# One PixArt-style chain on one core: normalisation, key/value and maxima steps moved in two hand-written turn tables

## The chip, the core and the metric

The kernel runs on one core of a Trainium2 chip. The metric is the device time of the whole program in microseconds; three runs of the kernel before took 2682.87, 2684.73 and 2690.53 us, the median is 2684.73. TensorE (PE) multiplies into PSUM, VectorE (DVE), ScalarE (ACT) and GpSimd (POOL) work beside it, and SyncE (SP) issues the DMAs. Each engine runs its own instructions in order and waits on semaphores for the others.

## The reference

The input x is (16, 256, 256): 16 samples of 256 tokens with 256 features, with a context of 120 tokens per sample and a condition vector. Four layers follow one another. Layers 0, 2 and 3 are full transformer blocks; layer 1 is a cross-attention alone. All is fp32, with 16 heads of 16 features:

```
full layer:                                       layer 1:
  shift, scale, gate = silu(cond) @ W_mod + b       q = (ada_ln(x) @ Wq + bq)
  x += gate * proj(self_attention(mod(ln(x))))      k, v = ada_ln(ctx) @ Wkv + bkv
  x += cproj(cross_attention(ln(x), ctx))           x += softmax(q k^T / 4) v @ Wp + bp
  x += gate * fc2(gelu(fc1(mod(ln(x)))))
```

In layers 1 and 3 the context is normalised before its keys and values are made; in 0 and 2 it is not. Layer 2 has a gain and a bias in the norm ahead of its cross-attention.

## The kernel before, in words

The weights of a layer and all of x stay in SBUF. The work is cut by layer and sample and laid out as a pipeline of jobs. The parts of a job are:

- **P**: normalise x (N, A), transpose it (LN), make q, k and v for self-attention (Q, K, V). RES adds a bias to x on GpSimd.
- **F**: self-attention. S0 to S3 compute scores, and VectorE takes each row's maximum from them (`row_max_F`, line 858). X splits the maxima in two parts, M transposes them on TensorE and ScalarE copies them out (`max_t_F`, line 983). T0 to T3 compute the scores again the other way round with the maxima subtracted, and ScalarE exponentiates (`probs`, line 994). PV0 to PV3 multiply by v, O0 and O1 divide by the sums on VectorE. **A** is the output projection (PR).
- **R**: normalise x for cross-attention (N, A, LN), transpose the context (C), make q (Q) and k and v (KV). NC and AC normalise the context in the layers that want it. **G** is the cross-attention, with S0, S1, T0 and T1 only; **B** is its projection.
- **E**: normalise (N, A, LN), fc1 and gelu (H0 to H3), fc2 (F20, F21a, F21b).

N is statistics on VectorE (`stats`, `mean_var`, `var_eps`, lines 718 to 726) and a power on GpSimd (`rstd`, line 671); A applies them (`x_hat`, line 733). A word such as `R.N` in a table is one step, and a step gives each engine its own piece: P.Q is matmuls on TensorE (line 1115), the high part of the result on ScalarE (line 976), the low part on VectorE (line 741), and four DMAs on SyncE which lay it out for F. Every engine walks the same list of steps. So a table sets the order of all five engines at once. Its last line holds loads and stores.

The table `TURN` is used once per turn i; in turns 3 to 21 it is the table `WITH_L1`, which carries layer 1 too (words that start with 1). `AHEAD` says which job a part works on in turn i: P i+1, F i, R and A i-1, G i-2, B and e (the norm of E) i-3, E i-4, 1p i-4, 1R i-5, 1G and 1B i-6; p, f and c are steps of P, F and R at another distance. Jobs 0 to 47 are the 16 samples of the three full layers, so F runs from turn 0 to turn 47, and a drain follows. Turns 6 to 20 are called layer-1 turns here, and turns from 22 on plain turns.

What TensorE waits for (lines 1014 to 1237 are its matmuls):

- `score` has one user at a time. Before an S or T step TensorE waits for the drain of the S or T step before it: its row maximum on VectorE, or its exponential on ScalarE.
- Three PSUM banks are a ring for all other results (`RING = 3`). A ring step waits for the drain of the third ring step before it.
- `k_parts` and `q_parts` are one buffer each. ScalarE may write them again when the DMAs of the step before have landed.
- `G.T0` also needs `max_t_G`, and `R.LN` needs `x_hat_R`.

Of the kernel before, what the change touches and what calls it, by code (L numbers as in the profile page):

```python
# [1265 lines left out]
```

How the kernel before makes its waits and increments, by code:

```python
    def wait_before(self, eng, m, n, back=1, k=None):  # L158
        earlier = self.order[m, n] - back
        if earlier >= 0:
            eng.wait_ge(self.sem, earlier * self.per + (self.per if k is None else k + 1))
# [363 lines left out]
            def load_tables(m):  # L526
                if m == 0:
                    sp.dma_start(cond, a["cond_1024"][0:nb, :]).then_inc(cond_loaded, 16)
                else:
                    sp.wait_ge(cols_psum, m)
                for at, v in row_vectors(m):
                    sp.dma_start(rows[at:at + v.shape[0] // P, :], v.rearrange("(n p) -> n p", p=P))\
                        .then_inc(rows_loaded, 16)
                if m > 0:
                    sp.wait_ge(mods_psum, m)
                    sp.wait_ge(gates_psum, FULL_BEFORE[m])
                if FULL[m]:
                    weight(w_ada[:, :, :], w(m, "ada_w"), ada_loaded)
                    if FULL_BEFORE[m] > 0:
                        sp.wait_ge(gate_times_bias, FULL_BEFORE[m])
                    ab = w(m, "ada_b").rearrange("(g d) -> g d", d=D)
                    for i, v in enumerate((ab[2], w(m, "proj_b"), ab[5], w(m, "fc2_b"))):
                        sp.dma_start(bias_rows[0:nb, i, :], v.unsqueeze(0).to_broadcast([nb, D]))\
                            .then_inc(gate_bias_loaded, 16)
                else:
                    weight(w_ada[:, :, 0:2 * D], w(m, "ss_q"), ada_loaded)
                    weight(w_ada[:, :, 2 * D:4 * D], w(m, "ss_kv"), ada_loaded)
```

## Time and profile before

| | us |
|---|---|
| three runs | 2682.87, 2684.73, 2690.53 |
| the profiled execution: its time, its span | 2690.53, 2688.7 |
| TensorE matmul busy | 2513.9 (93%) |
| VectorE, ScalarE, GpSimd busy | 1849.4, 1253.9, 454.9 |
| a layer-1 turn, a plain turn (F.S0 to F.S0) | 62.60, 47.40 |

The mean granted clock of TensorE is 0.975 of full. A row of a timeline has the start, the length (of the whole group, where several instructions stand together), the engine and the line, what is written and read, and in square brackets how long the engine had been idle and what ended that. All transposes on TensorE have line 1014, and the names tell them apart. In a turn F.S0 is the first of four groups `score<-k_F,q_F`.

### The profile page before, as it was taken

The numbers are of one execution on the slowest core, as the hardware profiler recorded it, in microseconds if no ns is written. First come the engines' busy times: TensorE is split into PE (matmuls) and PEld (weight loads), VectorE is DVE, ScalarE is ACT, GpSimd is POOL, SyncE is SP. The second block draws the span as 40 slices with busy tenths as digits, with TensorE's granted clock in tenths as the row PEclk, the third lists the DMA queues.
The fourth block names the chain that finished last, engine by engine and source line by source line (L and its number), as shares of the span: only waits on it lengthen the run. The fifth ranks groups of instructions, "written<-read, shape, count | busy, mean of one in ns | idle before, by whom it ended". The sixth has DMA issues, their size and how long they took to land.

```text
span 2688.7 us, 66128 instructions
## 1 busy us (share of the span) xinstructions
PE 2513.9 (93%) x27522; PEld 1888.4 (70%) x27522; DVE 1849.4 (69%) x3543; ACT 1253.9 (47%) x1759; POOL 454.9 (17%) x461
## 2 busy tenths in 40 slices
PE   6779899999999999999999999999999999999988
PEld 5546677777777777777677777777777777777766
DVE  3466677777777777777776766777777777777742
ACT  0233555444444455555545445454454545445442
POOL 0011211111121111111111111111211121111111
PEclk7688999999999999999999999999999999999999
DMA  5232222222222223232121212122131222313210
GB/s 183 80 97 64 81 76 71 80 81 81 71 71 75 80 71 97 71 103 74 51 75 62 86 51 89 57 89 84 62 114 61 88 71 67 92 55 94 64 40 28
DMA packets 236651, 207.54 MB, mean 77 GB/s; under 512 B 87634, under 2 KB 221972, under 8 KB 236356
## 3 DMA queue, kind: packets, MB, share of 16 engines
q1 hardware_dynamic: 236356, 203.32, 24.1%
q8 instruction: 220, 3.60, 0.6%
q14 instruction: 75, 0.61, 0.1%
HBM read 58.34 MB, written 4.39 MB: 23 GB/s over the span
## 4 chain that ended last, share of the span: by engine, by line
PE 76%; DVE 12%; issue 6%; ACT 5%; DMA 1%; SPq 1%; POOL 0%; POOLq 0%; DVEq 0%; ACTq 0%
PE ring L1237 12%; PE ring L1227 10%; PE ring L1115 10%; PE o_acc L1205 9%; PE score L1153 9%; PE score L1175 7%; PE ring L1217 5%; DVE row_max_F L858 4%; PE ring L1014 4%; DVE row_max_G L858 4%; PE ring L1123 3%; PE ring L1134 2%; PE score L1180 2%; ACT probs L994 2%; PE ring L1137 2%
## 5 line engine op out<-in xcount | busy, mean ns | idle before, releaser
L994 ACT ACTIVATE probs<-score 120x2048 f32<-120x2048 f32 (+1 forms) x320 | 602.1, 1881 | 258.9 <-PE score L1180 249.4
L858 DVE TENSOR_REDUCE row_max_F<-score 128x8 f32<-128x2048 f32 x192 | 438.0, 2281 | 63.7 <-PE score L1153 63.5
L1227 PE MATMUL ring<-x_t_E,w_fc 128*128 128x256 f32 x1536 | 379.3, 391 | 0.0
L1237 PE MATMUL ring<-w_fc,h_t 128*128 128x256 f32 x1536 | 363.0, 388 | 1.0 <-ACT h_t L1005 1.0
L1005 ACT ACTIVATE h_t<-ring,cols 128x256 f32<-128x256 f32 x384 | 161.2, 471 | 423.6 <-PE ring L1227 423.6
L1237 PEld LDWEIGHTS ring<-w_fc,h_t 128*128 128x128 f32 x1536 | 284.7, 191 | 59.4 <-issue 17.8
L1227 PEld LDWEIGHTS ring<-x_t_E,w_fc 128*128 128x128 f32 x1536 | 277.2, 189 | 67.4 <-issue 19.1
L858 DVE TENSOR_REDUCE row_max_G<-score 128x16 f32<-128x1920 f32 x128 | 276.0, 2157 | 51.5 <-PE score L1153 51.5
L880 DVE STREAM_TRANSPOSE o_turned<-o_acc 128x512 f32<-128x512 f32 x224 | 159.5, 712 | 125.5 <-PE o_acc L1205 123.8
L1205 PE MATMUL o_acc<-probs,v_self 128*17 128x256 f32 x3072 | 209.9, 391 | 1.0 <-ACT probs L994 1.0
L1115 PE MATMUL ring<-x_t_P,w_qk 128*128 128x256 f32 x768 | 194.4, 398 | 2.7 <-ACT x_t_P L946 2.5
L1153 PE MATMUL score<-k_F,q_F 32*128 32x256 f32 x3072 | 147.1, 308 | 51.0 <-DVE row_max_F L858 36.9
L741 DVE SCALAR_TENSOR_TENSOR q_parts<-ring,cols,q_parts 128x256 fp32r<-128x256 f32 x224 | 98.2, 480 | 136.1 <-ACT q_parts L976 136.1
L1153 PEld LDWEIGHTS score<-k_F,q_F 32*128 32x128 f32 x3072 | 107.1, 189 | 115.0 <-DVE row_max_F L858 69.9
L1175 PE MATMUL score<-q_F,k_F 32*128 32x256 f32 x3072 | 168.3, 306 | 13.5 <-ACT probs L994 10.2
L1153 PEld LDWEIGHTS score<-k_G,q_G 32*128 32x128 f32 x4096 | 127.0, 189 | 63.8 <-DVE row_max_G L858 44.4
L1115 PEld LDWEIGHTS ring<-x_t_P,w_qk 128*128 128x128 f32 x768 | 143.7, 197 | 33.6 <-issue 14.9
L1175 PEld LDWEIGHTS score<-q_F,k_F 32*128 32x128 f32 x3072 | 120.0, 186 | 66.6 <-issue 38.7
L1153 PE MATMUL score<-k_G,q_G 32*128 32x120 f32 x4096 | 144.6, 279 | 23.5 <-DVE row_max_G L858 23.5
L976 ACT ACTIVATE k_parts<-ring,cols 128x256 fp32r<-128x256 f32 (+1 forms) x224 | 79.5, 406 | 184.8 <-PE ring L1115 100.5
L912 DVE TENSOR_TENSOR gated_E<-ring,gate_now_E 128x256 f32<-128x256 f32 x96 | 40.8, 425 | 159.8 <-PE ring L1237 159.8
L741 DVE SCALAR_TENSOR_TENSOR k_parts<-ring,cols,k_parts 128x256 fp32r<-128x256 f32 (+1 forms) x224 | 79.7, 398 | 94.2 <-ACT k_parts L976 92.1
(133 smaller groups left out, 3856.1 us busy)
## 6 DMA issues: line engine op xcount, KB each, us to landing
q_G<-q_parts SPq DMA_DIRECT2D x256, 128.0 KB, 2.1
q_F<-q_parts SPq DMA_DIRECT2D x192, 128.0 KB, 2.1
k_F<-k_parts SPq DMA_DIRECT2D x96, 256.0 KB, 2.5
k_F<-k_parts SPq DMA_DIRECT2D x192, 128.0 KB, 2.2
k_G<-k_parts SPq DMA_DIRECT2D x128, 120.0 KB, 2.2
k_G<-k_parts SPq DMA_DIRECT2D x256, 60.0 KB, 1.9
gate_now_P<-gate_rows SPq DMA_DIRECT2D x48, 256.0 KB, 3.7
gate_now_E<-gate_rows SPq DMA_DIRECT2D x48, 256.0 KB, 3.8
```

Source lines behind the costliest of these rows:

```text
L741: last = nc.vector.scalar_tensor_tensor(out=parts[:, 1, c, 0:width].bitcast(F32R), in0=src[:, c * width:(c + 1) * width], scalar=row_col(m ...
L858: nc.vector.tensor_reduce(dst, src, AX.X, ALU.max).then_inc(row_max_ready[r].sem, 1)
L880: nc.vector.transpose(o_turned[:, :, :, :].rearrange("p i b d -> p (i b d)"), o_acc[:, :])\
L994: nc.scalar.activation(probs[v % 2][0:keys, :, :], score[0:keys, :].rearrange("p (h q) -> p h q", h=2 * GROUPS), ACT.Exp, scale=SCALE).the ...
L1005: last = nc.scalar.activation(h_t[:, c, :], ps[:, c % 2 * NT:(c % 2 + 1) * NT], ACT.Gelu_apprx_tanh, bias=col(m, "fc1", c))
L1115: last = mm(ps[:, c * NT:(c + 1) * NT], weight[:, k, at + c * P:at + (c + 1) * P], x_t[r][:, k, :], start=k == 0, stop=k == KC - 1)
L1153: last = mm(score[:, col0:col0 + width], q_now[at, c, e, tile * P:(tile + 1) * P].bitcast(F32R), k_now[at, two, c, e, :].bitcast(F32R), st ...
L1175: mm(score[0:keys, g * BANK + e * NT:g * BANK + (e + 1) * NT], k_now[at, two, c, e, tile * P:tile * P + keys].bitcast(F32R), q_now[at, c, ...
L1205: last = mm(o_acc[32 * j:32 * j + HD + 1, i * NT:(i + 1) * NT], v_head, probs[v % 2][0:keys, 2 * j + i, :], start=tile == 0 and (i == 0 or ...
L1217: last = mm(ps[:, t * D:(t + 1) * D], o_t[r][:, k, t * P:(t + 1) * P], weight[:, k, :], start=k == 0, stop=k == KC - 1)
L1227: last = mm(ps[:, c % 2 * NT:(c % 2 + 1) * NT], w_fc1[:, k, c * P:(c + 1) * P], x_t[r][:, k, :], start=k == 0, stop=k == KC - 1)
L1237: last = mm(ps[:, 0:D], h_t[:, k, t * P:(t + 1) * P], w_fc2[:, k, :], start=k == 0, stop=k == MC - 1)
```

## The change

Only the two tables and two dictionaries change; no step is added or taken out, and each does what it did. In the plain table R.N and R.A go up beside G.S0 and G.S1, R.C goes ahead of R.LN, G.M goes from F.T0 to behind R.LN, the norm of E with its LN moves up, E.F21a and E.F21b go from F.T3 to F.T2, and R.KV goes from F.T2 to F.T3, the last place. In the layer-1 table the norm for layer 1 goes from the end of a turn (as 1p) to the first three rows of the next (as 1R, for the same samples), R.N goes ahead of 1G.S1, R.A ahead of G.S0, e.N ahead of G.S1, and 1G.M and G.M one matmul step later and earlier.

```
--- before.py
+++ after.py
@@ -48,45 +48,45 @@
 F.S1 E.H1 P.V P.RES
 F.S2 E.H2 P.LN
 F.S3 F.X E.H3 A.PR
-G.S0 F.M B.PR E.RES
-G.S1 G.X E.F20 R.N
-F.T0 G.M P.Q R.A R.RES e.N
-F.T1 F.PV0 R.LN R.C e.A
-G.T0 F.PV1 F.O0 P.K p.N
-G.T1 G.PV0 G.O0 R.Q p.A c.NC
-F.T2 G.PV1 G.O1 R.KV e.LN c.AC
-F.T3 F.PV2 E.F21a E.F21b
+G.S0 F.M B.PR R.N E.RES
+G.S1 G.X E.F20 R.A e.N
+F.T0 P.Q R.C e.A R.RES
+F.T1 F.PV0 R.LN G.M e.LN p.N
+G.T0 F.PV1 F.O0 P.K p.A
+G.T1 G.PV0 G.O0 R.Q c.NC
+F.T2 G.PV1 G.O1 E.F21a E.F21b c.AC
+F.T3 F.PV2 R.KV
 P.ld c.ld P.gld E.gld P.ST
 """.split()
 WITH_L1 = """
-F.S0 f.PV3 f.O1 E.H0
-F.S1 E.H1 P.V P.RES
-F.S2 E.H2 P.LN
+F.S0 f.PV3 f.O1 E.H0 1R.NC
+F.S1 E.H1 P.V P.RES 1R.N 1R.AC
+F.S2 E.H2 P.LN 1R.A
 F.S3 F.X E.H3 A.PR 1R.RES
-1G.S0 F.M 1R.LN P.Q E.RES
-1G.S1 1G.X B.PR 1R.C R.N
-G.S0 E.F20 1G.M R.A R.RES
-G.S1 G.X P.K
-1G.T0 E.F21a e.N
-1G.T1 1G.PV0 1G.O0 E.F21b G.M e.A
-F.T0 1G.PV1 1G.O1 1R.Q p.N
-F.T1 F.PV0 1R.KV p.A
+1G.S0 F.M 1R.LN P.Q R.N E.RES
+1G.S1 1G.X B.PR 1R.C R.A
+G.S0 E.F20 R.RES e.N
+G.S1 G.X P.K 1G.M e.A
+1G.T0 G.M E.F21a p.N
+1G.T1 1G.PV0 1G.O0 E.F21b p.A
+F.T0 1G.PV1 1G.O1 1R.Q
+F.T1 F.PV0 1R.KV
 G.T0 F.PV1 F.O0 1B.PR
 G.T1 G.PV0 G.O0 R.LN R.C e.LN
-F.T2 G.PV1 G.O1 R.Q 1p.NC 1p.N
-F.T3 F.PV2 R.KV 1p.AC 1p.A
+F.T2 G.PV1 G.O1 R.Q
+F.T3 F.PV2 R.KV
 P.ld 1R.ld c.ld P.gld E.gld P.ST
 """.split()
 
 AHEAD = {"P": 1, "p": 2, "F": 0, "f": -1, "A": -1, "R": -1, "c": 0, "G": -2, "B": -3, "e": -3, "E": -4,
-         "1p": -4, "1R": -5, "1G": -6, "1B": -6}
+         "1R": -5, "1G": -6, "1B": -6}
 
 WORD_AHEAD = {"P.ld": 3, "c.ld": 1, "1R.ld": -3, "P.gld": 1, "E.gld": -3, "P.V": 0, "P.RES": 0, "P.ST": -4}
 FULL_LAYERS = [m for m in range(LAYERS) if FULL[m]]
 CROSS = "RGB"
 
 L1_TURNS = (3, 22)
-ROLE = {"p": "P", "f": "F", "c": "R", "e": "E", "1p": "R", "1R": "R", "1G": "G", "1B": "B"}
+ROLE = {"p": "P", "f": "F", "c": "R", "e": "E", "1R": "R", "1G": "G", "1B": "B"}
 
 RING_STEPS = ("LN", "C", "Q", "K", "V", "KV", "M", "PR", "H0", "H1", "H2", "H3", "F20", "F21a",
               "ZT", "ZC", "ZM", "ZG")
```

VectorE at the start of a layer-1 turn (`stats_C` and `x_hat_C` are the context, `stats_R` and `x_hat_R` are x, both for layer 1). Before, from the context's statistics to F.S0's maximum:

```order
L718 BN_STATS stats_C<-room 120x6
L723 BN_AGGR mean_var_C<-stats_C 120x2
L726 TENSOR_SCALAR var_eps_C<-mean_var_C 120x1
L718 BN_STATS stats_R<-x11 128x6 x2
L723 BN_AGGR mean_var_R<-stats_R 128x2 x2
L726 TENSOR_SCALAR var_eps_R<-mean_var_R 128x2
L741 SCALAR_TENSOR_TENSOR k_parts<-ring0,cols0,k_parts 128x120 x2
L842 TENSOR_TENSOR v_ctx1<-ring0,vc_bias 120x16x16
L733 TENSOR_SCALAR x_hat_C<-room,mean_var_C,rstd_C 120x256
L733 TENSOR_SCALAR x_hat_R<-x11,mean_var_R,rstd_R 128x256 x2
L858 TENSOR_REDUCE row_max_F<-score 128x4x2
```
After, from the end of O1 to 1R.A:

```order
L891 STREAM_TRANSPOSE o_t_A<-o_norm 128x256
L718 BN_STATS stats_C<-room 120x6
L723 BN_AGGR mean_var_C<-stats_C 120x2
L726 TENSOR_SCALAR var_eps_C<-mean_var_C 120x1
L858 TENSOR_REDUCE row_max_F<-score 128x4x2
L832 TENSOR_TENSOR v_self<-ring0,v_bias 128x32x16
L718 BN_STATS stats_R<-x11 128x6 x2
L723 BN_AGGR mean_var_R<-stats_R 128x2 x2
L726 TENSOR_SCALAR var_eps_R<-mean_var_R 128x2
L733 TENSOR_SCALAR x_hat_C<-room,mean_var_C,rstd_C 120x256
L858 TENSOR_REDUCE row_max_F<-score 128x4x2
L733 TENSOR_SCALAR x_hat_R<-x11,mean_var_R,rstd_R 128x256 x2
```
The context's statistics have moved between the first and the second maximum, the statistics of x and `x_hat_C` between the second and the third, and `x_hat_R` behind the third.

VectorE in the middle of a layer-1 turn; the first row is the maximum of 1G.S0, `stats_R` is here the R part of a full layer. Before:

```order
L858 TENSOR_REDUCE row_max_G<-score 128x16
L741 SCALAR_TENSOR_TENSOR q_parts<-ring1,cols2,q_parts 128x256 x2
L858 TENSOR_REDUCE row_max_G<-score 128x16
L867 TENSOR_SCALAR max_parts_G<-row_max_G 128x8x4
L870 SCALAR_TENSOR_TENSOR max_parts_G<-row_max_G,max_parts_G 128x8x4
L904 TENSOR_TENSOR x13<-ring2,x13 128x512
L718 BN_STATS stats_R<-x15 128x6 x2
L723 BN_AGGR mean_var_R<-stats_R 128x2 x2
L726 TENSOR_SCALAR var_eps_R<-mean_var_R 128x2
L858 TENSOR_REDUCE row_max_G<-score 128x16
```
After:

```order
L858 TENSOR_REDUCE row_max_G<-score 128x16
L741 SCALAR_TENSOR_TENSOR q_parts<-ring1,cols2,q_parts 128x256 x2
L718 BN_STATS stats_R<-x15 128x6 x2
L723 BN_AGGR mean_var_R<-stats_R 128x2 x2
L726 TENSOR_SCALAR var_eps_R<-mean_var_R 128x2
L858 TENSOR_REDUCE row_max_G<-score 128x16
L867 TENSOR_SCALAR max_parts_G<-row_max_G 128x8x4
L870 SCALAR_TENSOR_TENSOR max_parts_G<-row_max_G,max_parts_G 128x8x4
L904 TENSOR_TENSOR x13<-ring2,x13 128x512
L733 TENSOR_SCALAR x_hat_R<-x15,mean_var_R,rstd_R 128x256 x2
L858 TENSOR_REDUCE row_max_G<-score 128x16
```
The statistics of R now stand ahead of the second maximum, that of 1G.S1, and `x_hat_R` ahead of the third, that of G.S0.

ScalarE in a plain turn whose R part is in layer 2; the first exponential is F.T0's, the third G.T0's. Before:

```order
L994 ACT_TABLE_LOAD
L994 ACTIVATE probs0<-score 128x2048
L983 ACTIVATE max_t_G<-ring2 128x256
L976 ACTIVATE q_parts<-ring0,cols3 128x256 x2
L994 ACTIVATE probs1<-score 128x2048
L946 ACTIVATE x_t_R<-ring1,cols2 128x256 x2
L953 ACTIVATE context_t<-ring2 128x240
L994 ACTIVATE probs0<-score 120x2048
```
After:

```order
L994 ACT_TABLE_LOAD
L994 ACTIVATE probs0<-score 128x2048
L976 ACTIVATE q_parts<-ring2,cols3 128x256 x2
L953 ACTIVATE context_t<-ring0 128x240
L994 ACTIVATE probs1<-score 128x2048
L946 ACTIVATE x_t_R<-ring1,cols2 128x256 x2
L983 ACTIVATE max_t_G<-ring2 128x256
L946 ACTIVATE x_t_E<-ring0,mods2 128x256 x2
L994 ACTIVATE probs0<-score 120x2048
```
The copy of G's maxima, `max_t_G`, stood ahead of the exponential of F.T1; now it stands behind that and behind `x_t_R`. `x_t_E` has come up from the end of the turn.

## Rows read from the trace of the kernel before

**Rows 1.** Part 1 of the page: busy us (share of the span), instructions
```profile
PE 2513.9 (93%) x27522; PEld 1888.4 (70%) x27522; DVE 1849.4 (69%) x3543; ACT 1253.9 (47%) x1759; POOL 454.9 (17%) x461
```

**Rows 2.** Windows of a layer-1 and a plain turn: length, busy, clock, DMA
```profile
784.94:847.54 62.60, 59.37 (x695) 44.50 (x694) 46.96 (x90) 31.04 (x44) 11.00 (x12) 1.00 0.25 76
1962.95:2010.35 47.40, 46.45 (x514) 34.92 (x514) 33.89 (x65) 23.55 (x33) 8.94 (x9) 1.00 0.30 94
```

**Rows 3.** Timeline, layer-1 turn, start: start us, us, engine, line, work
```profile
784.88 0.75 PE L1153 MATMUL score<-k_F,q_F 32*128 32x256 f32 x16
...
786.48 0.41 DVE L733 TENSOR_SCALAR x_hat_C<-context,mean_var_C,rstd_C 120x256 f32<-120x256 f32 x1
...
786.80 0.73 DVE L733 TENSOR_SCALAR x_hat_R<-x,mean_var_R,rstd_R 128x256 f32<-128x256 f32 x2
...
787.44 2.29 DVE L858 TENSOR_REDUCE row_max_F<-score 128x8 f32<-128x2048 f32 x1
...
789.79 0.74 PE L1153 MATMUL score<-k_F,q_F 32*128 32x256 f32 x16 [1.24 <-DVE row_max_F L858]
```

**Rows 4.** Timeline, VectorE in the same turn: second maximum, v_self, third maximum
```profile
791.50 2.25 DVE L858 TENSOR_REDUCE row_max_F<-score 128x8 f32<-128x2048 f32 x1
794.22 0.69 DVE L832 TENSOR_TENSOR v_self<-ring,v_bias 128x512 f32<-128x512 f32 x1 [0.46 <-PE ring L1123]
794.90 2.29 DVE L858 TENSOR_REDUCE row_max_F<-score 128x8 f32<-128x2048 f32 x1
```

**Rows 5.** Timeline, TensorE in the same turn: F.S2 and F.S3
```profile
794.11 0.74 PE L1153 MATMUL score<-k_F,q_F 32*128 32x256 f32 x16
...
797.25 0.75 PE L1153 MATMUL score<-k_F,q_F 32*128 32x256 f32 x16
```

**Rows 6.** Timeline, end of that turn: statistics of context and x
```profile
845.42 0.42 DVE L718 BATCH_NORM_STATS2 stats_C<-room 120x6 f32<-120x256 f32 x1
...
846.16 0.74 DVE L718 BATCH_NORM_STATS2 stats_R<-x 128x6 f32<-128x256 f32 x2
```

**Rows 7.** Timeline, middle of the layer-1 turn, around G.S0
```profile
806.93 2.15 DVE L858 TENSOR_REDUCE row_max_G<-score 128x16 f32<-128x1920 f32 x1
...
809.13 1.11 PE L1153 MATMUL score<-k_G,q_G 32*128 32x120 f32 x32 [0.74 <-DVE row_max_G L858]
...
810.11 0.74 DVE L718 BATCH_NORM_STATS2 stats_R<-x 128x6 f32<-128x256 f32 x2
...
811.25 2.16 DVE L858 TENSOR_REDUCE row_max_G<-score 128x16 f32<-128x1920 f32 x1
```

**Rows 8.** Timeline, 1G.T0 to 1G.T1 in the layer-1 turn
```profile
817.11 0.84 ACT L976 ACTIVATE k_parts<-ring,cols 128x256 fp32r<-128x256 f32 x2 [2.58 <-PE ring L1115]
...
817.41 0.51 PE L1175 MATMUL score<-q_G,k_G 32*120 32x256 f32 x8 [0.34 <-DVE row_max_G L858]
...
817.97 1.28 ACT L994 ACT_TABLE_LOAD   x1
...
819.26 1.88 ACT L994 ACTIVATE probs<-score 120x2048 f32<-120x2048 f32 x1
...
821.19 0.50 PE L1175 MATMUL score<-q_G,k_G 32*120 32x256 f32 x8 [0.87 <-ACT probs L994]
```

**Rows 9.** Timeline, plain turn, R in layer 3: F.T1 to G.T0
```profile
1990.49 1.88 ACT L994 ACTIVATE probs<-score 128x2048 f32<-128x2048 f32 x1
...
1992.11 0.63 PE L1014 MATMUL ring<-ident,x_hat_R 128*128 128x128 f32 x4 [0.68 <-DVE x_hat_R L733]
...
1992.78 0.66 ACT L946 ACTIVATE x_t_R<-ring 128x256 f32<-128x256 f32 x2 [0.41 <-PE ring L1014]
...
1992.88 0.50 PE L1175 MATMUL score<-q_G,k_G 32*120 32x256 f32 x8
...
1993.32 0.38 ACT L953 ACTIVATE context_t<-ring 128x240 f32<-128x240 f32 x1
```

**Rows 10.** Timeline, plain turn, R in layer 2: x_t_R
```profile
1517.88 1.02 ACT L946 ACTIVATE x_t_R<-ring,cols 128x256 f32<-128x256 f32 x2 [0.41 <-PE ring L1014]
```

## The prediction

> **What bounds the kernel now.** I read the page's busy line first: TensorE matmuls fill 93% of the span, VectorE 69%, ScalarE 47% [rows 1]. So the time is TensorE's work plus its holes, and a table that only reorders steps can only change the holes. Then the windows of single turns, from one F.S0 to the next. A turn that also carries layer 1 takes 62.60 us with 59.37 of matmul; a plain turn takes 47.40 with 46.45, both at a granted clock of 1.00 [rows 2]. Most turns repeat these two: 15 full ones of the first kind (turns 6 to 20) and 26 of the second (22 to 47, the last running into the drain). The program's edges cost more but hold few turns. Last, the timelines inside the two kinds, where the reader is to look at the square brackets on TensorE's rows: they give the hole and who ended it. The layer-1 turn has three big ones: 1.24 us before F.S1 for the first maximum [rows 3], 0.74 before G.S0 for 1G.S1's maximum [rows 7], and 0.34 and 0.87 before 1G.T0 and 1G.T1 [rows 8]. The plain turn has one, 0.68 before R.LN, for x_hat_R [rows 9].
>
> What makes the holes: one score tile of PSUM is shared by all S and T steps. TensorE may not write the next S step until VectorE has read the last one, 2.15 to 2.29 us a time, nor the next T step until ScalarE has exponentiated, 1.88 us. In the S part VectorE's maxima stand almost wall to wall; in the T part VectorE has air. Whatever the new table puts between two S steps on VectorE therefore delays a maximum.
>
> **The change part by part, layer-1 turn.** I keep the clock of the turn that starts at 784.88 and move rows.
>
> F.S0 to F.S1. Of the four pieces of layer 1's normalisation, x_hat_C and x_hat_R stood before the first maximum, from 786.48 to 787.44, 0.96 us [rows 3]. They leave, the maximum starts at 786.48, and the hole shrinks from 1.24 to 0.28: F.S1 at 788.83. But 1R.NC now stands before the second maximum: stats_C to stats_R is 0.74 [rows 6]. That maximum started at 791.50 [rows 4], now 791.50 - 0.96 + 0.74 = 791.28, and ends 2.25 later at 793.53. F.S1 to F.S2 is 4.32 us of matmul when nothing waits (789.79 to 794.11 [rows 3, 5]), so TensorE is there at 793.15, and waits to 793.6: 0.45 lost.
>
> F.S2 to F.S3. VectorE does v_self (0.68 from start to start [rows 4]), then the whole of 1R.N (stats_R to the maximum behind it, 810.11 to 811.25, 1.14 [rows 7]) and x_hat_C (0.32, from its start to x_hat_R's [rows 3]): 793.50 + 0.68 + 1.14 + 0.32 = 795.64 for the third maximum, which then ends at 797.93. TensorE could have had F.S3 at 793.60 + 3.14 (794.11 to 797.25 [rows 5]) = 796.74; it gets it at 797.98 instead of 797.25. The turn is now 0.73 behind, where removing x_hat had put it 0.96 ahead. 1R.A after it costs nothing more: F.X, E.H3 and A.PR cover the last maximum.
>
> 1G.S0 to G.S0. R.N moves from behind G.S0 to ahead of 1G.S1's maximum. That maximum started at 806.93 with no idle time before it, directly behind the low part of Q [rows 7], so nothing hides R.N: 806.93 + 0.73 + 1.14 = 808.80. From its start to G.S0 was 2.20 (809.13 - 806.93 [rows 7]), so G.S0 comes at 811.00, not 809.13: 1.87 behind, a hole of about 1.9 where there was 0.74. R.A also goes before G.S0's maximum and e.N before G.S1's, but E.F20's 16 matmuls give these room; and 1G.M's two transposes leave the path, 0.3 (six take 0.77, below), so G.S1 comes 1.6 late.
>
> G.S1 to 1G.T1. 1G.M moves to behind P.K. On ScalarE the copy of the maxima then stands behind the high part of K: 817.11 + 1.6 = 818.71 and 0.84 long, of which the next step overlaps some 0.1; the copy (0.38, as rows 9 have one) runs from 819.46 to 819.84, and 1G.T0 goes at 819.9 instead of 817.41 [rows 8], a hole of 1.0 (was 0.34). The table load follows: it ran 817.97 to 819.25 and 1G.T1 came 3.22 after its start. From 819.85 this gives 823.07 for 821.19. G.M, which stood between 1G.T1 and F.T0, has moved ahead, 0.3 fewer: F.T0 is 1.57 late. From there both tables have the same order without holes, so **each layer-1 turn is 1.6 us longer**, 64.2. 15 x 1.57 = 23.6, and turns 5 and 21, which have half the layer-1 work, some 1.5 together: **+25 us**. Ends: 0 if the added VectorE work found room that I do not see, and 2.9 a turn (1.14 + 0.74 + 1.0, every added piece in full) or 46 us.
>
> On the table load ScalarE's row shows probs starting at 819.26, 0.01 us after the load's end [rows 8]. The Trainium skill, in "ScalarE: Activation LUTs", section "What ACT_TABLE_LOAD costs", says that a drain of 1380 ns follows the 1283 ns load. By that rule 1G.T1 would come 1.38 later than I have it and the time some 21 us longer; the trace has the 1283 but no room for the drain, and the row decides.
>
> **The plain turn.** R.N and R.A go early, so the 0.68 before R.LN goes. They cost nothing there: R.N (1.14) delays G.S1's maximum, but F.T0, which waits for it, stands behind E.F20's sixteen matmuls. What is late next is G.T0. G.M now comes after F.T1, and ScalarE takes its steps in order: the exponential of F.T1 ends at 1992.37 [rows 9], then x_t_R, 0.54 from its start to the next step's (1992.78 to 1993.32), then the copy of G's maxima, 0.38 like the context's: it ends at 1993.2 and G.T0 can go at 1993.27. TensorE would be ready at 1992.7 (R.LN at 1992.11 - 0.68, then ten transposes; six took 0.77, 1992.11 to 1992.88 [rows 9]). Hole 0.57. In layer 2 x_t_R has scale and bias columns and takes 1.02 instead of 0.66 [rows 10]: hole 0.93. ScalarE's old slack, with G.M before F.T1, is gone.
>
> The tail of the plain turn now ends in R.KV as the layer-1 turn's did. There v_ctx stands until 786.5, so the first maximum starts 1.6 after F.S0 and leaves the 0.28 hole worked out above; the plain turn had none. The gate load for P.RES is issued behind R.KV's DMAs and so later too, and P.RES with it; A.PR's long way through the S part hides that. Sum: -0.68 + 0.57 + 0.28 = +0.17 where R is in layer 3, +0.53 in layer 2; 15 x 0.17 + 11 x 0.53 = **+8 us**. Ends: -0.68 x 26 = -18 if ScalarE's queue does not bind, and +1.2 x 26 = +31 if both holes come in full with none given back.
>
> **Edges.** In the drain x_hat_R no longer holds R.LN up; I take 2 us off (three turns at 0.68), between 0 and -5. The sum is 25 + 8 - 2 = +31. The profiled execution took 2690.53 us (span 2688.7); the median of the three runs is 2684.73, 5.8 lower. The shift is put on the median: **2716 us**, 1.2% slower.
>
> **Rivals.** *It gets faster, because waits on x_hat go and nothing replaces them.* Place: VectorE in the S part. If the maxima had 1.14 us of slack behind the Q step (the deciding point), each layer-1 turn would give 0.96 and each plain one 0.68: 15 x 0.96 + 26 x 0.68 = 32 off, 2653. For it: VectorE is only 69% busy. Against it: the maximum at 806.93 has no idle time before it and TensorE waits on it already. *Holes only swap places.* The added 0.45 + 0.7 + 1.1 is real but ScalarE and VectorE regain it in the T part, where the exponentials have had slack; time 2685. Against it: the T part after F.T0 has no TensorE hole to give back. *Only layer-1 turns lose*, with ScalarE's copy in time in the plain turn: +25 - 26 x 0.4 - 2 = +13, 2698. *More is lost:* a late POOL add meets x_hat or o_norm on VectorE, or a drain as in the rule above, +20 on top, 2736. *The table does not do what it says* is out: the order on the engines shows it done.
>
> **How the numbers follow.** The forecast (2705 to 2730) gets 0.58; only layer 1 loses 0.14; more lost 0.10; holes swap 0.10; faster 0.08. About 0.3%, 8 us, is what a measurement can tell from no change. Faster 0.08, within 0.3% 0.10, slower 0.82. The range 2688 to 2742 takes in all cases but the faster one and part of the swap.
>
> **What would show it.** Layer-1 turns of about 64.2 us and plain ones of 47.6 (layer 3) and 47.9 (layer 2). TensorE's hole before F.S1 falls to 0.3; new ones of 0.45 before F.S2, 1.2 before F.S3, 1.9 before G.S0, 1.0 before 1G.T0, all but the last released by a maximum. In plain turns the x_hat_R wait is gone and one of 0.6 to 0.9 before G.T0 is released by max_t_G. Unchanged F.S3 and G.S0 holes would make the forecast wrong; so would plain turns of 46.8.

## The result and the profile after

| | before | after |
|---|---|---|
| median of the runs on one chip | 2685.4 (2682.87 to 2690.53) | 2757.49 (2750.43 to 2760.08) |
| span of the profiled execution | 2688.7 | 2757.3 |
| mean granted clock of TensorE | 0.975 | 0.968 |

The median of before is here that of four runs, the three named at the start and one of 2686.07. The changed kernel is slower, at a ratio of means of 1.0257 over all its runs (95% interval 1.0238 to 1.0276). By the medians it takes 72 us more, where the prediction had 31. The direction was right, the size was off by a factor of more than two, and the time lies outside the range of 2688 to 2742.

The busy line of the page of after, which answers to [rows 1]:

```profile
PE 2537.3 (92%) x27522; PEld 1902.8 (69%) x27522; DVE 1835.5 (67%) x3543; ACT 1253.7 (45%) x1759; POOL 456.9 (17%) x461
```

The count of matmuls is the same and their busy time has grown by 23.4 us. A reordering adds no matmul, so the matmuls themselves have become slower somewhere. That is the first sign of what the prediction missed: it looked for holes alone.

What TensorE waits for, after (engine, line and tile <- engine and work waited for: us, times, longest):

```profile
PE score L1153 <- DVE row_max_F L858: 57.1, 87, 2.3
PE score L1153 <- DVE row_max_G L858: 44.9, 49, 3.9
PE score L1175 <- ACT max_t_G L983: 38.5, 42, 1.1
...
PE ring L1014 <- DVE x_hat_E L733: 9.3, 3, 3.4
```

And the same view of before:

```profile
PE score L1153 <- DVE row_max_F L858: 36.9, 35, 3.4
...
PE score L1153 <- DVE row_max_G L858: 23.5, 47, 3.0
PE ring L1014 <- DVE x_hat_R L733: 21.6, 28, 3.2
...
PE ring L1014 <- DVE x_hat_E L733: 3.4, 1, 3.4
```

The wait for `x_hat_R` is gone (1.0 us is left), 20.2 and 21.4 us have come at the two kinds of row maxima, and `max_t_G` has 38.5, where it had 0.6 in before. These are the exchanges that the prediction named. The wait for `probs` has fallen to 23.3 from 34.5: the hole of 0.87 before 1G.T1 is no longer there, as the prediction's times for 1G.T0 and 1G.T1 imply. The wait for `x_hat_E` has grown by 5.9: that is the drain.

The start of a layer-1 turn after (start, length, engine, line, work, idle time before it), VectorE and TensorE, which answers to [rows 3 to 5] (F.S0 is at 739.81):

```profile
743.75 0.75 PE L1153 MATMUL score<-k_F,q_F 32*128 32x256 f32 x16 [0.27 <-DVE row_max_F L858]
...
748.51 0.74 PE L1153 MATMUL score<-k_F,q_F 32*128 32x256 f32 x16 [0.37 <-DVE row_max_F L858]
...
750.11 0.41 DVE L733 TENSOR_SCALAR x_hat_C<-room,mean_var_C,rstd_C 120x256 f32<-120x256 f32 x1
...
750.44 2.29 DVE L858 TENSOR_REDUCE row_max_F<-score 128x8 f32<-128x2048 f32 x1
...
752.78 0.74 PE L1153 MATMUL score<-k_F,q_F 32*128 32x256 f32 x16 [1.17 <-DVE row_max_F L858]
```

F.S1 waits 0.27 us (forecast 0.28), F.S2 0.37 (0.45), F.S3 1.17 (1.2). The middle of the same turn, which answers to [rows 7, 8]:

```profile
762.45 0.74 DVE L718 BATCH_NORM_STATS2 stats_R<-x 128x6 f32<-128x256 f32 x2
...
763.59 2.15 DVE L858 TENSOR_REDUCE row_max_G<-score 128x16 f32<-128x1920 f32 x1
...
765.79 1.11 PE L1153 MATMUL score<-k_G,q_G 32*128 32x120 f32 x32 [1.88 <-DVE row_max_G L858]
...
774.82 0.50 PE L1175 MATMUL score<-q_G,k_G 32*120 32x256 f32 x8 [1.08 <-ACT max_t_G L983]
```

G.S0 waits 1.88 behind the maximum that `stats_R` has pushed back (forecast 1.9), 1G.T0 1.08 (1.0). Every hole of this layer-1 turn is where it was put, and within 0.1 us of its size.

Now windows, which answer to [rows 2]: three layer-1 turns of after, one of 64.1, one of 67.5 and one of 65.8 us, the whole stretch of turns 6 to 21, and a plain turn with R in layer 3 and one with R in layer 2:

```profile
740.00:804.10 64.10, 59.32 (x694) 44.33 (x695) 46.64 (x90) 30.74 (x45) 10.96 (x11) 1.00 0.24 73
804.10:871.60 67.50, 62.72 (x694) 46.93 (x698) 46.73 (x90) 30.83 (x45) 10.94 (x11) 0.95 0.23 71
414.20:480.00 65.80, 61.02 (x694) 45.59 (x696) 46.64 (x90) 30.77 (x45) 10.95 (x11) 0.97 0.23 72
346.60:1395.90 1049.30, 967.35 (x11019) 722.83 (x11018) 746.93 (x1432) 491.49 (x696) 173.25 (x173) 0.98 0.24 74
2212.70:2260.50 47.80, 46.58 (x511) 35.00 (x510) 33.55 (x65) 23.62 (x33) 9.04 (x9) 1.00 0.24 75
1444.00:1492.15 48.15, 46.57 (x511) 34.99 (x510) 32.66 (x61) 23.98 (x33) 8.42 (x8) 1.00 0.22 69
```

Turns 6 to 21 of before:

```profile
346.70:1345.50 998.80, 945.54 (x11015) 708.22 (x11014) 746.47 (x1424) 495.03 (x696) 172.80 (x172) 1.00 0.25 77
```

The reader should look at the matmul busy time and the granted clock together. With 694 to 696 matmul records a turn has 59.32, 61.02 or 62.72 us of matmul, at a clock of 1.00, 0.97 or 0.95: steps of 1.7 us. Over turns 6 to 21 it is 967.35 at 0.98 after and 945.54 at 1.00 before, 21.8 us more for the same work. The busy times of VectorE and GpSimd move by less than 0.5 us, and ScalarE's falls by 3.5. A closer look at one such stretch: four windows in a row around G.S0 of another turn:

```profile
565.60:567.20 1.60, 1.60 (x22) 1.41 (x19) 1.31 (x4) 0.26 (x1) 0.00 (x0) 1.00 0.00 0
567.20:570.60 3.40, 1.52 (x26) 1.17 (x28) 3.19 (x8) 0.79 (x2) 1.93 (x2) 1.00 0.47 154
570.60:574.00 3.40, 3.40 (x26) 2.75 (x23) 3.20 (x4) 0.00 (x0) 1.26 (x1) 0.53 0.02 5
574.00:577.40 3.40, 3.40 (x44) 2.79 (x42) 0.94 (x3) 0.00 (x0) 0.00 (x0) 0.97 0.00 0
```

In the second window TensorE is busy for 1.52 of 3.40 us; that is where the hole before G.S0 lies. In the third it is fully busy, but at 0.53 of the clock, so nearly at 1.2 GHz instead of 2.4, and 26 matmuls fit where 44 fit in the fourth. Turns 6 to 21 have eleven such stretches after, of 3.4 or 6.8 us, and none before. Nine of the eleven begin at G.S0 or E.F20 right behind the hole; the other two begin in E.H3 of turns 19 and 20, behind F.S3's hole, which is 2.27 and 1.92 us long there.

### The profile page after: what moved, and what is told of

Read it like the earlier page. It is cut to its first block, busy times and chain, and to the rows that moved or that the text cites. A ratio compares the mean times of both kernels' runs of the same rounds, so it can differ in the third digit from the quotient of the medians.

```text
span 2757.3 us, 66128 instructions
## 1 busy us (share of the span) xinstructions
PE 2537.3 (92%) x27522; PEld 1902.8 (69%) x27522; DVE 1835.5 (67%) x3543; ACT 1253.7 (45%) x1759; POOL 456.9 (17%) x461
## 4 chain that ended last, share of the span: by engine, by line
PE 70%; DVE 17%; issue 6%; ACT 4%; DMA 1%; SPq 1%; POOL 1%; POOLq 0%; DVEq 0%; ACTq 0%
PE ring L1237 12%; PE ring L1115 11%; PE o_acc L1205 9%; PE score L1175 8%; DVE row_max_F L858 7%; PE score L1153 7%; PE ring L1227 7%; PE ring L1217 4%; DVE row_max_G L858 4%; PE score L1180 3%; PE ring L1134 3%; PE ring L1014 2%; PE ring L1137 2%; PE ring L1123 2%; ACT probs L994 1%
## 5 line engine op out<-in xcount | busy, mean ns | idle before, releaser
L858 DVE TENSOR_REDUCE row_max_F<-score 128x8 f32<-128x2048 f32 x192 | 437.9, 2281 | 42.1 <-PE score L1153 41.9
L1237 PE MATMUL ring<-w_fc,h_t 128*128 128x256 f32 x1536 | 375.3, 398 | 1.0 <-ACT h_t L1005 1.0
L1237 PEld LDWEIGHTS ring<-w_fc,h_t 128*128 128x128 f32 x1536 | 294.5, 198 | 62.0 <-issue 18.6
L1175 PE MATMUL score<-q_G,k_G 32*120 32x256 f32 x2048 | 112.7, 306 | 50.8 <-ACT max_t_G L983 38.5
```

What stands on the lines that cost most here:

```text
L858: nc.vector.tensor_reduce(dst, src, AX.X, ALU.max).then_inc(row_max_ready[r].sem, 1)
L1175: mm(score[0:keys, g * BANK + e * NT:g * BANK + (e + 1) * NT], k_now[at, two, c, e, tile * P:tile * P + keys].bitcast(F32R), q_now[at, c, ...
L1237: last = mm(ps[:, 0:D], h_t[:, k, t * P:(t + 1) * P], w_fc2[:, k, :], start=k == 0, stop=k == MC - 1)
```

## The experiments

All times below are medians. Each ratio is one of means, to the kernel before on the same chip, with its 95% interval. The median of before was 2686.55 us beside e1 to e4, 2684.9 beside e5, e6, e8 and e9, and 2685.98 beside e7, e10 and e11. Turns and stretches are read from one profiled execution of each kernel.

| run | us | ratio |
|---|---|---|
| e1, plain table alone | 2705.21 | 1.0071 [1.0054, 1.0087] |
| e2, layer-1 table alone | 2737.90 | 1.0194 [1.0178, 1.0209] |
| e3, holes filled with matmuls | 2735.26 | 1.0185 [1.0167, 1.0202] |
| e4, R.N and R.A back in the layer-1 table | 2729.16 | 1.0160 [1.0142, 1.0178] |
| e10, R.N alone moved | 2727.88 | 1.0162 [1.0144, 1.0181] |
| e5, layer 1's norm back at the end of a turn | 2746.84 | 1.0232 [1.0216, 1.0247] |
| e9, P.RES behind 1R.N | 2749.90 | 1.0252 [1.0234, 1.0269] |
| e6, G.M back in the plain table | 2731.12 | 1.0178 [1.0163, 1.0194] |
| e7, R.KV back in the plain table | 2747.78 | 1.0226 [1.0212, 1.0240] |
| e8, only the moves that pay | 2655.38 | 0.9891 [0.9876, 0.9906] |
| e11, e8 and G.M earlier | 2648.64 | 0.9865 [0.9852, 0.9879] |

### The two tables apart (e1, e2)

e1 is the kernel before with the new `TURN`, e2 the changed kernel with the old one. In e1 these rows change, among others of the same table, and in e2 they change back:

```
-G.S0 F.M B.PR E.RES                        +G.S0 F.M B.PR R.N E.RES
-G.S1 G.X E.F20 R.N                         +G.S1 G.X E.F20 R.A e.N
...
-F.T3 F.PV2 E.F21a E.F21b                   +F.T3 F.PV2 R.KV
```

> The plain table of after with the layer-1 table of before. Holes theory (time is matmul work plus holes, plus half-clock stretches that follow long holes): plain turns 47.8 (R in layer 3) and 48.15 us (layer 2) for 47.40, +12.7 us; drain +5; first turns -4; layer-1 turns stay at 62.60 with the clock at 1.00. About 2698 us. Rival, that half-clock stretches come with any run of the new order or with the chip and not with long holes: they show in the layer-1 turns here too, 2715 or more.

> The layer-1 table of after with the plain table of before. Holes theory: layer-1 turns 64.17 us where the clock stays at 1.00, +1.57 each (+24), half-clock stretches in about two of three of them (+20), x_hat_C caught beside POOL's add in a few (+5), turns 3 to 5 and 21 +6; plain turns back at 47.40. About 2738 us. Rival, that the two tables only lose together: 2710.

e1 gave 2705.21, 18.7 above before; e2 gave 2737.9, 51.4 above. Together 70, and the whole change is 72: the parts add up, and the layer-1 table carries nearly three quarters. e2 came at its expected 2738. e1 came 7 us above its 2698; in its trace the last turn and the drain are 7.8 us longer than before's, 3.3 of it in matmul busy time, where 5 was expected. Turns 6 to 21 and a plain turn of e1:

```profile
342.80:1341.50 998.70, 945.52 (x11015) 708.14 (x11014) 746.14 (x1424) 495.04 (x696) 172.78 (x172) 1.00 0.25 77
2158.40:2206.20 47.80, 46.59 (x515) 35.01 (x514) 33.54 (x65) 23.62 (x33) 9.03 (x9) 1.00 0.24 75
```

With the old layer-1 table the matmuls take 945.52 again. So the slower matmuls belong to the new layer-1 table.

### Is it the holes that bring the clock down? (e3)

The changed kernel, with the projection B done twice and P's transposes three times in the layer-1 turns. The repeated results overwrite the same values; some 39 us of matmul work is added, all of it just ahead of the holes at G.S0 and F.S3.

```
-  for k in range(KC): ... transpose(...)
+  for again in range(3 if r == "P" and 7 <= FULL_BEFORE[m] * nb + n <= 21 else 1):
+      for k in range(KC): ... transpose(...)
...
-  for t in range(TT): ... mm(... weight[:, k, :] ...)
+  for again in range(2 if r == "B" and m != 1 and 3 <= FULL_BEFORE[m] * nb + n <= 18 else 1):
+      for t in range(TT): ... mm(... weight[:, k, :] ...)
```

> After, with matmuls repeated in front of two holes in the layer-1 turns: B.PR's eight passes once more (1.7 us, before the 1.9 us hole at G.S0) and P.LN's four transposes twice more (0.9 us, before the 1.2 us hole at F.S3). They write the same values to the same bank. TensorE does about 39 us more work in all. Clock theory (the hole lets the granted clock fall to half right behind it): holes turn into work, no half-clock stretch in turns 6 to 21, turns 64.2 instead of 65.8 or more, 2737 us. Rival (the half clock has another cause, or the extra time is DMA or POOL traffic): nothing is regained, 2757 us, or more by what does not fit the holes.

It gave 2735.26, 22 us less than the change, with more work to do, and close to the 2737 that the clock theory expected. A turn of it:

```profile
415.40:479.60 64.20, 62.02 (x708) 46.84 (x707) 46.71 (x91) 30.91 (x44) 10.97 (x11) 1.00 0.23 70
```

And its way into G.S0 (line numbers are one or two higher):

```profile
559.83 1.67 PE L1219 MATMUL ring<-w_cp,o_t_B 128*128 128x256 f32 x7
561.35 0.37 PE L1014 MATMUL ring<-ident,x_hat_C 120*128 120x120 f32 x2
561.86 1.11 PE L1154 MATMUL score<-k_G,q_G 32*128 32x120 f32 x32
```

A turn is 64.2 us long, as the undisturbed ones of the change, since the maximum still sets when G.S0 may go. But TensorE works where it waited: the hole before G.S0 is down to some 0.14, the one before F.S3 to 0.29 in most turns. The clock is 1.00 from turn 6 to turn 21. So about 20 us of the change's loss are the clock, and it is idle time of TensorE that brings it down, not the new order as such.

### Which hole? (e4, e10, e5)

e4 puts R.N and R.A of the layer-1 table back. e10 goes the other way: the kernel before, with R.N alone moved ahead of the maximum of 1G.S1.

```
e4, against the change:                     e10, against before:
-1G.S0 F.M 1R.LN P.Q R.N E.RES              -1G.S0 F.M 1R.LN P.Q E.RES
-1G.S1 1G.X B.PR 1R.C R.A                   -1G.S1 1G.X B.PR 1R.C R.N
-G.S0 E.F20 R.RES e.N                       +1G.S0 F.M 1R.LN P.Q R.N E.RES
+1G.S0 F.M 1R.LN P.Q E.RES                  +1G.S1 1G.X B.PR 1R.C
+1G.S1 1G.X B.PR 1R.C R.N
+G.S0 E.F20 R.A R.RES e.N
```

> After, with R.N alone put back behind 1R.C and R.A behind E.F20 in the layer-1 table, so the hole before G.S0 shrinks from 1.9 to about 0.74. Theory that this hole alone brings the half clock: layer-1 turns 63.0 us and no half-clock stretches, -17 and -20: 2720 us. Rival, that the holes at F.S2 and F.S3 bring it as much: -17 only, half-clock stretches now inside E.H3 or A.PR: 2740 us.

> Before, with one step moved: R.N ahead of 1G.S1's maximum in the layer-1 table. All else is before's. Clock theory (one hole of 1.9 us at G.S0 is enough for the granted clock to fall behind it): layer-1 turns 63.7 us where the clock stays, +18 us in all, and half-clock stretches at about 25 us into half of these turns, +10 to +25 more: 2715 to 2730. Rival, that it takes the holes at F.S2 and F.S3 too: clock 1.00 in turns 6 to 20, 2703.

Turns 6 to 21 of e4, and one of its turns:

```profile
346.30:1367.40 1021.10, 953.22 (x11015) 710.16 (x11014) 749.16 (x1432) 491.43 (x696) 173.34 (x173) 0.99 0.25 76
727.50:790.98 63.48, 59.54 (x695) 44.41 (x694) 46.76 (x90) 30.80 (x44) 10.95 (x11) 1.00 0.24 75
```

Turns 6 to 21 of e10, and two turns in a row:

```profile
342.90:1383.10 1040.20, 968.72 (x11017) 725.02 (x11017) 747.73 (x1424) 495.03 (x696) 172.91 (x172) 0.98 0.24 74
795.60:859.33 63.73, 59.37 (x695) 44.49 (x694) 47.04 (x90) 31.03 (x44) 11.00 (x12) 1.00 0.24 75
859.30:924.70 65.40, 61.03 (x691) 45.67 (x690) 47.04 (x90) 31.03 (x44) 11.00 (x11) 0.97 0.23 69
```

e10 is the plainest of all: one word moved by one row costs 41.9 us. The 2727.88 lie inside what the clock theory expected, and the rival's 2703 is out. An undisturbed turn is 1.13 us longer (63.73 for 62.60), which is R.N's 1.14; fifteen of them are 17 us. Nearly all of the rest is 968.72 - 945.54 = 23.2 us of slower matmuls, and all the half-clock stretches of these turns begin behind the hole at G.S0. In e4, where that hole is back at 0.73, the matmul busy time is 953.22 - 945.54 = 7.7 us above before's. Some 5 of these are three half-clock stretches; the rest is 0.15 us a turn that an undisturbed turn of e4 has more (59.54 for 59.38). e4 took 9 us more than expected for two reasons that its trace shows. First, the stretches: two begin in E.H3 of turns 15 and 19, behind holes of 2.24 and 2.10 us before F.S3, and one begins in E.F21a of turn 15, behind a hole of 1.41 us before 1G.T0. So the hole at G.S0 is the main one, but not the only one that can bring the clock down. Second, 1G.T0 now waits 1.41 us, for a row maximum, where it waited 1.08 for `max_t_G`, so an undisturbed turn is 63.48 and not 63.0.

e5 is the changed kernel with layer 1's norm at the end of the turn, as before:

```
-F.S0 f.PV3 f.O1 E.H0 1R.NC                 +F.S0 f.PV3 f.O1 E.H0
-F.S1 E.H1 P.V P.RES 1R.N 1R.AC             +F.S1 E.H1 P.V P.RES
-F.S2 E.H2 P.LN 1R.A                        +F.S2 E.H2 P.LN
-F.T2 G.PV1 G.O1 R.Q                        +F.T2 G.PV1 G.O1 R.Q 1p.NC 1p.N
-F.T3 F.PV2 R.KV                            +F.T3 F.PV2 R.KV 1p.AC 1p.A
```

> After, with layer 1's norm back at the end of the turn (1p) as in before; the rest of both tables as in after. Holes theory: F.S1's hole back at 1.3 us, those at F.S2 (0.5) and F.S3 (1.2, and 2.0 to 2.3 in turns 15 to 20) gone; a layer-1 turn without half clock is 63.5 us; half-clock stretches behind the 1.9 us hole at G.S0 stay, those in H3 go. About 2738 us. Rival, that the sum of the holes of a turn and not the long one brings the half clock: none left in turns 6 to 20, 2725.

It gave 2746.84, 9 us above what was expected. Turns 6 to 21, an undisturbed turn, and one of the usual ones:

```profile
345.30:1386.20 1040.90, 971.37 (x11019) 726.25 (x11018) 744.18 (x1424) 490.94 (x696) 172.35 (x172) 0.97 0.24 74
606.20:669.77 63.57, 59.32 (x695) 44.42 (x694) 46.81 (x90) 30.77 (x44) 10.96 (x12) 1.00 0.24 74
735.00:800.21 65.21, 60.96 (x693) 45.63 (x693) 46.81 (x90) 30.78 (x44) 10.95 (x12) 0.97 0.24 73
```

The undisturbed turn came out as expected (63.57 for 63.5), so the sum over holes holds. But 14 of 15 turns have a half-clock stretch here, against 8 in the change, and slower matmuls make 25.8 us. That is the 9 us, for the hole at G.S0 is the same. Which of the turns with this hole are hit differs from kernel to kernel and no run explains it; in the profiled executions of the kernels with a hole of 1.9 us at this place (the change, e2, e5, e6, e7, e9, e10) it was 7 to 14 of turns 6 to 20. So a difference of a few us between two of these kernels can be such hits and not the order.

### GpSimd beside VectorE (e9)

In the change F.S3 waits longer in some turns. In turn 18 (F.S0 at 1131.6):

```profile
1141.99 1.47 DVE L733 TENSOR_SCALAR x_hat_C<-room,mean_var_C,rstd_C 120x256 f32<-120x256 f32 x1
1142.04 1.27 POOL L686 TENSOR_TENSOR x<-x,gate_now_P 128x512 f32<-128x512 f32 x1 [3.27 <-DMA gate_now_P<-gate_rows]
...
1143.38 2.28 DVE L858 TENSOR_REDUCE row_max_F<-score 128x8 f32<-128x2048 f32 x1
...
1145.71 0.51 PE L1153 MATMUL score<-k_F,q_F 32*128 32x256 f32 x8 [2.22 <-DVE row_max_F L858]
```

`x_hat_C` takes 1.47 us beside the addition of P.RES on GpSimd; alone it takes 0.41, and it ends only when the addition does. The maximum and F.S3 are one microsecond late. In turns 19 and 20 the addition falls on `var_eps_R`, one instruction earlier, which takes 1.28 and 0.93 us for 0.17. In the turns up to 14 it starts behind `x_hat_C`. e9 puts P.RES behind 1R.N in the step list of the change:

```
-F.S1 E.H1 P.V P.RES 1R.N 1R.AC
+F.S1 E.H1 P.V 1R.N P.RES 1R.AC
```

> After, with P.RES behind 1R.N in the layer-1 table, so that GpSimd does the short power first and the add (1.27 us) does not start ahead of VectorE's var_eps_R and x_hat_C. Shared-port theory (VectorE's two-port steps stand still while GpSimd's add runs): F.S3's hole is 1.2 us in all layer-1 turns, not 2.0 to 2.3 in turns 15 and 17 to 20, and the half clock in H3 of turns 19 and 20 goes: -5 to -9 us, 2750. Rival, that those turns are late for a DMA: holes of 2.0 stay, 2757.

It gave 2749.9 for an expected 2750. The time alone proves nothing, for the intervals of the two ratios overlap (1.0252 and 1.0257); the rows decide. The same place in its turn 18:

```profile
1133.35 0.41 DVE L733 TENSOR_SCALAR x_hat_C<-room,mean_var_C,rstd_C 120x256 f32<-120x256 f32 x1
...
1133.68 2.28 DVE L858 TENSOR_REDUCE row_max_F<-score 128x8 f32<-128x2048 f32 x1
...
1134.28 1.26 POOL L686 TENSOR_TENSOR x<-x,gate_now_P 128x512 f32<-128x512 f32 x1
...
1136.01 0.75 PE L1153 MATMUL score<-k_F,q_F 32*128 32x256 f32 x16 [1.17 <-DVE row_max_F L858]
```

The addition comes behind, `x_hat_C` has its 0.41 and F.S3 its 1.17 again, in turns 18, 19 and 20. Turn 18 alone would not show it, for e2, e4 and e6 have no such meeting there either; but in turns 19 and 20 all the kernels with P.RES in its old place and the new norm at the start (the change, e2, e4, e6, e7) have F.S3 holes of 1.87 to 2.27 us. In turns 15 and 17 F.S3 stays at 2.0, against the expectation, and the cause is another: copies of the next layer's weights stand on VectorE ahead of `v_self` there, as in turn 15 of the change:

```profile
945.85 0.91 DVE L764 COPY w_qk<-w_raw 128x256 f32<-128x256 f32 x4
```

No run moved these copies. The two half-clock stretches at E.H3 of turns 19 and 20 are gone as well, but that is not shown to be e9's doing: e7 has F.S3 holes of 2.05 and 1.87 us in these turns and no such stretch. The Trainium skill ("SBUF — State Buffer", section "SBUF: two separate sides") says that GpSimd and VectorE share a pair of ports, and that the instruction which gets it first holds it as an exclusive lock while the other is blocked. The pair of rows agrees in that `x_hat_C` ends only behind the addition; which of the two came first they don't decide, for their starts are 0.05 us apart.

### The plain turn (e6, e7)

e6 puts G.M back to the head of F.T0, e7 puts R.KV back to F.T2 and E.F21a and E.F21b to F.T3, both in `TURN` alone.

```
e6: -F.T0 P.Q R.C e.A R.RES                 e7: -F.T2 G.PV1 G.O1 E.F21a E.F21b c.AC
    -F.T1 F.PV0 R.LN G.M e.LN p.N               -F.T3 F.PV2 R.KV
    +F.T0 G.M P.Q R.C e.A R.RES                 +F.T2 G.PV1 G.O1 R.KV c.AC
    +F.T1 F.PV0 R.LN e.LN p.N                   +F.T3 F.PV2 E.F21a E.F21b
```

> After, with G.M alone put back in front of P.Q in the plain table. Theory that ScalarE's order makes the plain turn's new hole: no wait for max_t_G in plain turns, 47.1 us in layer 3 and 47.1 in layer 2 instead of 47.80 and 48.15, that is -22 us: 2735. Rival, that G.T0 would wait as long for the exponential of F.T1: plain turns stay, 2757.

> After, with R.KV back at F.T2 and E.F21a, E.F21b back at F.T3 in the plain table. Holes theory: F.S1's new hole (0.36 us, VectorE still at R.KV's low part and v_ctx when F.S0 ends) goes from 26 plain turns, -9 us: 2748. Rival, that ScalarE or the k_parts buffer then makes the turn late at another place (R.KV's high part waits for P.K's DMAs in before): plain turns stay at 47.80 and 48.15.

e6 gave 2731.12 us, where 2735 was expected, and e7 2747.78, where 2748 was. One plain turn of each (R in layer 3), e6 first:

```profile
2195.40:2242.48 47.08, 46.54 (x511) 34.88 (x510) 33.53 (x65) 23.41 (x33) 9.03 (x9) 1.00 0.25 76
```

```profile
2203.80:2251.25 47.45, 46.51 (x511) 34.99 (x510) 33.65 (x65) 23.62 (x33) 8.94 (x9) 1.00 0.24 76
```

Against the 47.80 of the change, G.M's place is worth 0.72 a turn and R.KV's 0.35. In both cases the hole itself is a little less, 0.68 before G.T0 and 0.27 before F.S1; the rest is matmul busy time. In layer 2 G.M's place is worth 1.05. In the change ScalarE's own rows show the first one:

```profile
2051.25 0.65 ACT L946 ACTIVATE x_t_R<-ring 128x256 f32<-128x256 f32 x2
2051.77 0.40 ACT L983 ACTIVATE max_t_G<-ring 128x256 fp32r<-128x256 f32 x1
...
2052.32 0.50 PE L1175 MATMUL score<-q_G,k_G 32*120 32x256 f32 x8 [0.68 <-ACT max_t_G L983]
```

The copy of G's maxima queues behind `x_t_R`, and G.T0 waits for it.

### What is worth keeping (e8, e11)

e8 is the kernel before with the moves that the experiments speak for, and with one place that the change did not have. In the plain table R.N and R.A go early and G.M stays. In the layer-1 table the norm for layer 1 stays at the turn's end, but ahead of R.Q and R.KV. e11 also moves G.M.

```
-G.S0 F.M B.PR E.RES                        +G.S0 F.M B.PR R.N E.RES
-G.S1 G.X E.F20 R.N                         +G.S1 G.X E.F20 R.A
-F.T0 G.M P.Q R.A R.RES e.N                 +F.T0 G.M P.Q R.RES e.N
-F.T2 G.PV1 G.O1 R.Q 1p.NC 1p.N             +F.T2 G.PV1 G.O1 1p.NC 1p.N R.Q
-F.T3 F.PV2 R.KV 1p.AC 1p.A                 +F.T3 F.PV2 1p.AC 1p.A R.KV
and in e11 also, in the layer-1 table:
-1G.T0 E.F21a e.N                           +1G.T0 G.M E.F21a e.N
-1G.T1 1G.PV0 1G.O0 E.F21b G.M e.A          +1G.T1 1G.PV0 1G.O0 E.F21b e.A
```

> Before, with two edits: in the plain table R.N behind B.PR and R.A behind E.F20, nothing else moved; in the layer-1 table 1p.AC and 1p.A ahead of R.KV, so that VectorE does x_hat_C and x_hat_R while TensorE is at R.KV. Holes theory: R.LN's hole (0.7 us in 26 plain turns) and 1.0 of F.S1's 1.3 in 16 layer-1 turns go, nothing new: 46.7 and 61.6 us a turn, 2652 us. Rival, that something else is then late by as much (context or rstd not ready at the end of the turn): 2685.

> The kernel of e8 with G.M in the layer-1 table between 1G.T0 and E.F21a, where TensorE has a hole of 0.9 us behind E.F21a for the exponential. Holes theory: G.M's 0.3 us go into that hole, 61.3 us a layer-1 turn instead of 61.6, -5 us against e8: 2650. Rival, that ScalarE's copy of the maxima then delays an exponential: 2655 or more.

They gave 2655.38 and 2648.64 us, for an expected 2652 and 2650. A layer-1 and a plain turn of e8, then a layer-1 turn of e11:

```profile
708.50:770.12 61.62, 59.37 (x691) 44.51 (x690) 46.80 (x90) 31.00 (x44) 10.98 (x11) 1.00 0.26 77
2121.80:2168.75 46.95, 46.47 (x511) 34.91 (x511) 33.54 (x65) 23.43 (x33) 8.96 (x9) 1.00 0.25 76
```

```profile
704.60:766.00 61.40, 59.30 (x695) 44.37 (x694) 46.73 (x90) 30.92 (x44) 10.99 (x11) 1.00 0.26 77
```

A plain turn of e8 is 46.95 and not the expected 46.7, since 0.20 us of a wait for `probs` before G.T0 comes in place of the 0.68 before R.LN. The 0.98 us a layer-1 turn is what the prediction said the removal of `x_hat` from ahead of the first maximum would give (0.96); the change had spent it again two rows later. e11 is the best version: 1.35% under before.

## Why the prediction was right in kind and wrong in size

The spans differ by 68.6 us. Cut at F.S0 of turns 6, 21, 22 and 47:

| stretch | forecast | measured |
|---|---|---|
| turns 0 to 5 | some 0.8 | 0 |
| turns 6 to 20, longer holes | 23.6 | 23.6 (15 x 1.57) |
| turns 6 to 20, half clock | 0 | 19.7 |
| turns 15, 17 to 20, F.S3 later still | 0 | 4.8 |
| turn 21 | some 0.8 | 2.7 |
| turns 22 to 46 (forecast with 47) | 8 | 12.7 |
| turn 47 and the drain | -2 | 5.5 |

The measured column adds up to 69.0; before has 0.4 of its own in turns 15, 17 and 18. The half-clock row is what the ten stretches of turns 6 to 20 add with the same holes. The 0 in the first row is no success: turn 5 is 2.1 us longer, and turns 0 to 4 happen to be as much shorter. Of turn 21's 2.7, 1.6 is one more half-clock stretch.

**The holes of the layer-1 turn: right.** Five holes were named with their sizes and releasers, and all five are in the trace within 0.1 us. The undisturbed turn is 64.17 as forecast; e5 and e10, which take or leave single moves, are 63.57 and 63.73 and fit the same sums. e4, at 63.48 for 63.0, fits them less well.

**The step that failed: "each layer-1 turn is 1.6 us longer", +25.** It priced a hole at its own length. The prediction had read a clock of 1.00 in both turns of before [rows 2] and carried it over to a turn with other holes. Measured, turns 6 to 20 are 47.7 us longer. The largest part that was missing is the clock, 19.7 us. e3 shows that idle time of TensorE is its cause (filled, it is gone), e10 that the move of R.N alone brings it (23.2 us of slower matmuls), e4 that most of it goes when R.N goes back (7.7, of which some 5 at half clock). How many turns are hit is not explained: with this hole the slower matmuls of turns 6 to 21 are 15.0 us in e9 and 25.8 in e5, so the runs give a range for the term and no single value. Before, the largest hole of the turn was 1.24, and no stretch of turns 6 to 21 was slowed.

**GpSimd against VectorE: a rival, not in the sum.** "A late POOL add meets x_hat" is what e9 shows, in turns 18 to 20, and it is some 3 us; the rival had priced it at 20. Its 2736 came nearer to the measured time than the forecast did, but the larger part of what was missing, the clock, is not in it. The other 1.6 us at F.S3 go with the weight copies of turns 15 and 17, which the prediction had not named. By the rows, the added work had used up VectorE's air, so 0.8 us of copies now reach TensorE, where before they cost 0.2.

**The plain turn: right mechanism, sized low.** 47.80 and 48.15 were measured for 47.57 and 47.93. F.S1's hole came as 0.27 for 0.28 (e7 takes it away), G.T0's as 0.68 for 0.57 in layer 3 and 1.03 for 0.93 in layer 2 (e6 takes it away). Part of that tenth is a slip of the sum: 1992.37 + 0.54 + 0.38 is 1993.29, where it has 1993.2. The other tenth a turn is matmul busy time, 46.58 for 46.45 at a clock of 1.00. It goes with the number of waits: e6 and e7, with one of the two holes each, have 46.54 and 46.51. Two tenths in each of 25 turns are the 5 us of difference.

**The drain: wrong sign.** x_hat_R did stop holding R.LN up there (3.2 to 1.0 us), as forecast. But the norm of E, which now comes earlier in the list, holds E.LN up: TensorE's wait for `x_hat_E` goes from 3.4 us in one place to 9.3 in three. No run moved the norm of E alone, but e1 and e2 place the loss in the plain table: with it (e1) the wait is 9.3 us and the last turn with the drain 7.8 us longer than before's, without it (e2) 3.4 and 0.8 shorter. Putting G.M (e6) or R.KV (e7) back changes neither by more than 1 us. e8 and e11, which leave e.LN and e.A where they were, have a drain 4 us shorter than before's.

**The other rivals.** *Holes only swap places*, *faster* and *only layer-1 turns lose* are excluded: e1 alone is slower by 18.7 us. A drain behind the table load, the other half of *more is lost*, did not come either: in the turn of after shown above 1G.T1 starts at 777.91, 3.09 us behind 1G.T0, where the prediction's own times have 3.17.

## What to carry to other kernels

Where one engine has all of its slack in one phase, read for each step moved which instruction it now stands ahead of: one norm of 1.14 us in front of a maximum that TensorE waits for cost 42 us over the layer-1 turns. Price a new hole on TensorE above its own length. If it is clearly longer than any hole of the kernel before, the granted clock read there says nothing about after, and the range must leave room for as much again: here 19.7 us came on top of 23.6. The sign is matmul busy time that grows by per cents with an unchanged count, together with a granted clock below 1.00. A growth of a few tenths of a per cent is no such sign: the plain turn has 0.13 us more at a clock of 1.00. And before adding VectorE work beside GpSimd's additions, look where those fall in every turn, not only in one.

## What the runs showed of the hardware

- TensorE's clock: holes of 1.88 us before G.S0 were followed in 7 to 14 of 15 turns, by kernel, by stretches of 3.4 or 6.8 us at a granted clock near a half, which is the level of 1.2 GHz. One of 3.4 us made a turn 1.6 to 1.7 us longer. With that hole filled (e3) or at 0.8 us or less (e8, e11), none came in turns 6 to 21. With it at 0.73, two came behind holes of 2.1 and 2.2 us before F.S3, and one behind a hole of 1.41 before 1G.T0 (e4).
- Adding matmuls made a kernel faster: e3 does some 39 us more of matmul than the change and takes 22 us less.
- A `TENSOR_SCALAR` of VectorE beside an addition on GpSimd: 1.47 us for 0.41 alone (the change, turn 18). A row maximum beside the same addition kept its 2.28 (e9, turn 18).
